# Four loops written out, the second batch's tokens fetched into idle buffers, and a last iteration that prepares nothing

## The reference

```
x = x + attn_a(layernorm(x), ...)   # 16 heads of 32, causal, biases on qkv and out
x = x + ffn(layernorm(x), ...)      # silu(x @ gate.T) * (x @ up.T) @ down.T, hidden 2048
x = x + attn_b(layernorm(x), ...)
x = x + ffn(layernorm(x), ...)
```

## Time and profile before

| | |
|---|---|
| median of 3 runs | 2034.46 us (2031.79 to 2035.56) |
| the profiled execution: its own time | 2035.76 us |
| its span, first to last instruction | 2034.0 us |
| instructions in the trace | 34492 |
| busy: PE, DVE, POOL, ACT | 1982.6, 1168.1, 999.4, 813.8 us |
| mean granted TensorE clock | 0.997 |

### The profile page before, as it was taken

The page is one execution under the profiler, slowest core; times in us unless marked ns, Lnnn a source line. Parts: engine busy times, 40 slices in busy tenths (PEclk is TensorE's granted clock), DMA queues, the critical chain, the costliest instruction groups (busy, mean ns, idle before and its releaser), DMA issues.

```text
span 2034.0 us, 34492 instructions
## 1 busy us (share of the span) xinstructions
PE 1982.6 (97%) x10304; PEld 1442.5 (71%) x10304; DVE 1168.1 (57%) x2404; ACT 813.8 (40%) x1481; POOL 999.4 (49%) x775
## 2 busy tenths in 40 slices
PE   7999999999999999999999999999999999999998
PEld 5555588888755558888765555888887555688887
DVE  4767555445577755454457775545456767544454
ACT  2388522221158742222115874222221676432221
POOL 4224359753312437975331243797533223389743
PEclk9999999999999999999999999999999999999999
DMA  4333111111333310111243331111113333111112
GB/s 150 90 79 90 33 42 54 51 63 42 85 75 85 74 43 32 62 53 52 73 136 75 85 75 43 32 63 52 52 43 85 74 84 75 43 42 63 53 53 83
DMA packets 59177, 134.07 MB, mean 66 GB/s; under 512 B 10720, under 2 KB 11744, under 8 KB 58976
## 3 DMA queue, kind: packets, MB, share of 16 engines
q1 hardware_dynamic: 58976, 131.66, 23.0%
HBM read 76.57 MB, written 4.19 MB: 40 GB/s over the span
## 4 chain that ended last, share of the span: by engine, by line
PE 89%; issue 3%; ACT 3%; DVE 2%; DMA 2%; POOL 0%; SPq 0%; DVEq 0%; ACTq 0%; POOLq 0%
PE bank L1306 11%; PE bank L1308 11%; PE bank L1307 11%; PE bank L1442 10%; PE ring L1306 10%; PE ring L1307 10%; PE ring L1308 10%; PE bank L1415 8%; PE ring L1384 7%; PE ring L1297 1%; ACT masked L831 1%; DMA area<-nm_lo 1%; ACT prob L809 1%; DMA x<-x_in 1%; DVE xn L1039 0%
## 5 line engine op out<-in xcount | busy, mean ns | idle before, releaser
L809 ACT ACTIVATE prob<-bank 128x512 f32<-128x512 f32 (+1 forms) x512 | 271.9, 571 | 143.5 <-PE bank L1415 115.1
L611 POOL TENSOR_SCALAR area<-w_stage 128x1024 fp32r<-128x1024 f32 x129 | 139.5, 1082 | 366.8 <-PE bank L1308 206.3
L688 POOL TENSOR_SCALAR_AFFINE_SELECT prob<-prob 128x512 f32<-128x512 f32 x128 | 82.9, 648 | 479.5 <-ACT prob L809 339.8
L613 POOL TENSOR_TENSOR area<-w_stage,area 128x1024 fp32r<-128x1024 f32 x129 | 309.2, 2397 | 10.8
L1110 DVE TENSOR_TENSOR x<-x,bank 128x512 f32<-128x512 f32 x256 | 171.1, 685 | 234.3 <-PE bank L1308 233.1
L1039 DVE CUSTOM_DVE_ANT_0 xn<-ring,mask_row 128x384 bf16<-128x384 f32 (+7 forms) x384 | 246.3, 661 | 86.7 <-PE ring L1384 84.4
L1306 PE MATMUL ring<-xt_hi,area 128*128 128x512 f32 x672 | 266.3, 396 | 1.6 <-DVE area L1143 1.0
L1307 PE MATMUL ring<-xt_lo,area 128*128 128x512 f32 x672 | 262.9, 391 | 0.0
L1308 PE MATMUL ring<-xt_hi,area 128*128 128x512 f32 x672 | 262.6, 391 | 0.0
L1415 PE MATMUL bank<-area 98*128 98x512 f32 (+3 forms) x768 | 247.8, 380 | 7.1 <-DMA area<-nm_lo 3.9
L1384 PE MATMUL ring<-area 96*128 96x512 f32 (+3 forms) x768 | 227.4, 362 | 9.9 <-DVE row_max L1039 5.5
(11 more groups left out here) (166 smaller groups left out, 3626.5 us busy)
## 6 DMA issues: line engine op xcount, KB each, us to landing
w_stage<-ffn_w SPq DMA_DIRECT2D x96, 512.0 KB, 3.3
area<-kq_parts SPq DMA_DIRECT2D x336, 128.0 KB, 2.3
w_stage<-attn_w SPq DMA_DIRECT2D x35, 512.0 KB, 3.3
area<-attn SPq DMA_DIRECT2D x48, 128.0 KB, 2.3
x<-x_in SPq DMA_DIRECT2D x20, 256.0 KB, 3.9
out<-x SPq DMA_DIRECT2D x16, 256.0 KB, 2.5
bias_rows<-row_bias SPq DMA_DIRECT2D x10, 256.0 KB, 4.4
area<-nm_hi SPq DMA_DIRECT2D x32, 8.0 KB, 1.8
```

Source lines behind the costliest of these rows:

```text
L611: pool.tensor_scalar(hi, src, 1.0, 0.0, ALU.mult, ALU.add).then_inc(w_hi_done, 1)
L613: pool.tensor_tensor(lo, src, hi.bitcast(F32), ALU.subtract).then_inc(w_split, 1)
L809: act.activation(prob[:, step % PROB_BUFS, h, off:], scores_at(u, j, h), ACT.Exp, scale=SCALE).then_inc(prob_ready, 1)
```

## The change

1. The loops over iterations are written out on all engines, so that every wait compares with a constant; `wait_alone` is gone, and each of its waits is a plain one, without the extra wait for `const_ready`.
2. Before it loads slot 18 of iteration 1, SP fetches all eight token tiles of the second batch into `masked` (six tiles) and `prob[:, 1]` (two tiles). The statistics and the normalisation of iteration 2's first layer norm read these copies. `x` itself is still reloaded behind the stores; POOL waits for it before it adds the output bias.
3. Iteration 3 loads no further weights or biases, reloads no `x`, and makes no statistics, transposes, splits or ones for a following iteration.

```diff
+LAST = BATCH * LAYERS - 1
+STAGE_BEFORE = 18
...
+        def staged_tile(t):
+
+            return masked[:, t // 2, t % 2 * DIM:(t % 2 + 1) * DIM] if t < 2 * MASKED_BUFS else prob[:, 1, t - 2 * MASKED_BUFS, :]
+
+        def first_layer(it):
+
+            return it % LAYERS == 0
+
+        def source_tile(it, t):
+
+            return staged_tile(t) if it and first_layer(it) else x[:, t, :]
...
-        def wait_alone(eng, semaphore, value):
...
+            def stage_x(it, batch):
+                sp.wait_ge(row_summed, it * SUM_TILES + SUM_TILES + MASKED_BUFS)
+                sp.wait_ge(pv_done, it * KEY_STEPS + KEY_STEPS)
+                for t in range(TT):
+                    sp.dma_start(staged_tile(t), x_in[batch, t * P:(t + 1) * P, :]).then_inc(x_staged[t // CT], 16)
...
-                with sp.Fori(0, LAYERS) as layer:
+                for layer in range(0, LAYERS):
...
+                    if it < LAST:
+                        sp.wait_ge(out_bias_added, it * TT + TT)
+                        load_biases(1 - layer)
+                    for i in range(12, SLOTS + (AHEAD if it < LAST else 0)):
+                        if i == STAGE_BEFORE and it < LAST and first_layer(it + 1):
+                            stage_x(it, b + 1)
...
-                        if n >= AFTER_STORE and not (b == BATCH - 1 and c):
+                        if n >= AFTER_STORE and b < BATCH - 1:
...
+                for s in x_loaded if first_layer(it) else ():
+                    pool.wait_ge(s, (it // LAYERS + 1) * (16 * CT))
...
-                wait_alone(pool, prob_ready, it * S2_STEPS + GH * (step + 1))
+                pool.wait_ge(prob_ready, it * S2_STEPS + GH * (step + 1))
...
+                if it == LAST:
+                    return
...
-                act.preload_act_table_set(EXP_TABLE)
-
-                xt_to_hi(it + 1, ("ln1", 0))
-                xt_to_hi(it + 1, ("ln1", 1))
+                if it < LAST:
+                    act.preload_act_table_set(EXP_TABLE)
+                    xt_to_hi(it + 1, ("ln1", 0))
+                    xt_to_hi(it + 1, ("ln1", 1))
...
+                if it == 0:
+                    dve.wait_ge(x_loaded[c], 16 * CT)
+                elif first_layer(it):
+                    dve.wait_ge(x_staged[c], it // LAYERS * (16 * CT))
                 for t in range(c * CT, (c + 1) * CT):
-                    tile_stats(t)
+                    tile_stats(t, source_tile(it, t))
...
-                dve.wait_ge(rows_drained, rows_taken(it, ROWS - CT - 1))
-                chunk_stats(it + 1, 0, b + layer + 1)
+                if it < LAST:
+                    dve.wait_ge(rows_drained, rows_taken(it, ROWS - CT - 1))
+                    chunk_stats(it + 1, 0)
...
-            with pe.Fori(0, BATCH * LAYERS) as it:
+            for it in range(BATCH * LAYERS):
                 iteration(it)
```

More of the change, by code:

```diff
@@ L310, in block_kernel @@
         x_loaded = [sem(f"x_loaded{c}") for c in range(CHUNKS)]
+        x_staged = [sem(f"x_staged{c}") for c in range(CHUNKS)]
         x_stored = [sem(f"x_stored{t}") for t in range(TT)]
@@ L495, in load_weights @@
                 if i >= 2 or it is not None:
-                    wait_alone(sp, w_split, (0 if it is None else it * SLOTS) + i - 1)
+                    sp.wait_ge(w_split, (0 if it is None else it * SLOTS) + i - 1)
                 j = i % SLOTS
@@ L598, in split_weights @@
                     if after[0] == "product":
-                        wait_alone(pool, product_full, products(it, *after[1:]))
+                        pool.wait_ge(product_full, products(it, *after[1:]))
                     elif after[0] == "rows":
-                        wait_alone(pool, rows_full, it * ROWS + after[1] + 1)
+                        pool.wait_ge(rows_full, it * ROWS + after[1] + 1)
                     elif after in SIDE:
-                        wait_alone(pool, side_full, side_done(it, after))
+                        pool.wait_ge(side_full, side_done(it, after))
                     else:
-                        wait_alone(pool, ring_full, full(it, after))
+                        pool.wait_ge(ring_full, full(it, after))
                 elif place(j) in LENT_PLACES:
                     lent_steps = KEY_STEPS if place(j) == 0 else J_BASE[6]
-                    wait_alone(pool, s2_full, it * S2_STEPS + GH * lent_steps)
+                    pool.wait_ge(s2_full, it * S2_STEPS + GH * lent_steps)
                 hi, lo, src = *w_part(j, slice(0, SLOT)), w_stage[:, j % 2, :]
@@ L722, in _, with iteration @@
                 split_weights(0, i)
-            with pool.Fori(0, BATCH * LAYERS) as it:
+            def iteration(it):
                 inverse_deviation(it, 0, 1)
@@ L750, in _ @@
                 inverse_deviation(it, 1, 1)
-                wait_alone(pool, xn_ready, it * 2 * TT + 2 * TT)
-                for i in range(FFN_SLOT0 + 3, SLOTS + 2):
+                pool.wait_ge(xn_ready, it * 2 * TT + 2 * TT)
+                for i in range(FFN_SLOT0 + 3, SLOTS + (2 if it < LAST else 0)):
                     if i == DIFFS_AT:
-                        wait_alone(pool, ring_drained, drained(it, ("ln2", 3)))
+                        pool.wait_ge(ring_drained, drained(it, ("ln2", 3)))
                         for n in range(6):
@@ L765, in _ @@
                     split_weights(it, i)
+            for it in range(BATCH * LAYERS):
+                iteration(it)
         @block.scalar
@@ L958, in _ @@
             xt_to_hi(0, ("ln1", 1))
-            with act.Fori(0, BATCH * LAYERS) as it:
+            for it in range(BATCH * LAYERS):
                 iteration(it)
@@ L1004, in xt_to_lo, with iteration @@
                 ins.then_inc(ring_drained, 1)
-            def iteration(it, b, layer):
+            def iteration(it):
                 def take_v(t):
@@ L1279, in _ @@
             xt_to_lo(0, 0, 1)
-            with dve.Fori(0, BATCH) as b:
-                with dve.Fori(0, LAYERS) as layer:
-                    iteration(b * LAYERS + layer, b, layer)
+            for it in range(BATCH * LAYERS):
+                iteration(it)
         @block.tensor
```

99 lines of the change are left out of this document (50 added, 49 removed).

## The result

The changed kernel takes 2010.95 us (median of 5 runs, 2009.98 to 2012.1), beside 2034.46 us for the kernel before (5 runs, 2031.79 to 2036.66): a ratio of 0.9887, 95% interval 0.9873 to 0.99, so 1.1% faster. The forecast was 2016.0 us in a range of 2010 to 2025. The sign and the range hold, and the gain is 23.5 us where 18.5 were worked out.

The account below looks back on a forecast made before the run. TensorE was taken as the bound, busy 1982.6 of 2034.0 us. Terms 8.3 + 5.4 + 0.8 + 4.0 = 18.5 us off the profiled 2035.8 give 2017.3, less 1.3 to the median: 2016.0 us, range 2010 to 2025.

Parts of the forecast that it names:

- The second boundary: Iteration boundary where the second batch starts: staged tokens take the `x` reload off the path, 8.3 us off (7.8 to 8.9).
- the cover that was named: POOL adds the output bias only behind slot 3's split; slot 18 lands with 2.7 us to spare: both cost nothing.
- The last iteration: End of iteration 3: without the stall, transposes and splits, the last addition ends some 6.3 us after gate and up, 5.4 off.
- The jumps: Loop branches at iteration boundaries: PE gains 0.8 us at the first and third; the middle one is in the 8.3.
- The waits: Hand-overs with constant wait values: maxima, SP and POOL gain, exponentials lose; 4 us off, bounds 9 off and 5 on.
- The maxima: DVE's row maxima: the wait for scores sits on the operation, 0.11 us sooner at 44 chain hand-overs, 4.8 us off.
- The exponentials: ACT's exponentials: the later of two waits is set apart, 0.06 us later at 20 chain hand-overs, 1.2 us on.
- The register instructions: Instructions for register values in the loops: not shown as PE's bound anywhere, so given nothing.
- the stacking on SP and POOL's masks: Split of the maxima and its copy on SP, 1.0 us off; POOL's masks, four times 0.1 us off.
- the waits give more: Rival: half of DVE's 162 waits for scores count fully, ACT pays nothing; 9 us off, 2009 to 2012 us; 9%.
- slower: Rival: the instruction set apart delays every exponential, at all 512 wide ones 31 us on, 2047 us; 4%.

Follow-up runs that it names:

- loops_plain: The kernel before with its loops written out and its waits in ordinary form, without token copies, last iteration still preparing a next one: 2022.79 us, ratio 0.9938.
- no_copies: The changed kernel without the early token fetches, iteration 2's first layer norm reading the reloaded `x` as before: 2018.8 us, ratio 0.9914.
- last_prepares: The changed kernel whose last iteration again makes all preparations for a next one, but with no reload of `x` ahead of them: 2013.45 us, ratio 0.9892.
- maxima_alone: The changed kernel with DVE's wait for the scores set apart again ahead of the row maxima: 2013.65 us, ratio 0.9894.
- loops_alone: The kernel before with only its loops written out; `wait_alone` stays, with constants as values: 2030.18 us, ratio 0.997.
- exps_again: The changed kernel with the two waits of each exponential exchanged, scores first and free buffer second: 2007.60 us, ratio 0.9869.

## Why the prediction was right, and where it was short

**The second boundary: right.** 8.3 us were worked out. 508.62 has become 497.43, 11.2 less, and the other two intervals fell by 2.9 on average, which leaves 8.2. By the matmuls it is 9.0, of which loops_plain shows 1.0 without the copies. no_copies gives 6.6 to 7.9 back, with the clock low for half as long in its profiled execution. POOL's wait for `x` and the fetch of the copies cost nothing, with the cover that was named.

**The last iteration: right.** 5.4 us were forecast and 5.35 measured, closer than the working earned: the last addition was put 6.3 us behind gate and up and is 6.57 behind, which makes 5.1, and the tail behind it, which was taken to stay as it was, gave 0.3. last_prepares splits the 5.1 into 2.1 and 3.0.

**The jumps: small, as the row on PE said.** 0.9 and 0.5 us, 1.4 together, at the first and third boundary against 0.8 for both; 3 × 3.31 us did not come. The Trainium skill ("Runtime: NRT & Kernel Launch", Instruction fetch mechanics) has every far taken branch stall until its page is fetched: DVE's gap of 3.31 us is gone with the branch, which agrees, and PE hid most of it.

**The waits: right in kind, too small by more than half.** The term was 4.0 us; the traces show 6.7 in attention and 3.4 in the seven-product step, 10.1 together, beyond even its bound of 9. Its parts:
- The maxima: 4.8 us before the 80%, and maxima_alone gives 4.3 by the matmuls. That the two are so close is partly luck, since the 44 pieces that were counted at 0.11 us are not of one form: 20 are a lone wait as at 57.74, 16 stand beside a register instruction, and in 8 only the 0.02 us is on the chain.
- The exponentials: +1.2 forecast, 2.8 to 3.8 measured. The chain of the kernel before had 20 such hand-overs, and the number that pays is about 55 (3.3, the middle of the two, divided by 0.06): the chain shows those that were last already, and not those that become last when each is later.
- The register instructions: "I give them nothing" is the sentence that failed. I looked for them at PE; they stood on DVE, among the 44 hand-overs that I had counted: 12 times between wait and maximum, at 0.15 us each beyond the lone wait, 1.8 us, and 4 times ahead of a wait. Attention's balance asks for more: 6.7 gained, 4.3 of it the maxima, and 3.3 lost on ACT leave 5.7 us for registers, the stacking on SP and POOL's masks, for which 1.4 was forecast. loops_alone, with registers gone and exponentials already late, gained 1.3 net, so the registers may be 4 to 5 of these. That division is argued from single executions and is not isolated.
- POOL's waits in its sums and weight splits: not looked for. Their rows were in the timeline of before (0.43 us of idle time between two sums), but POOL is busy 49% of the time, and I took its own lateness as harmless. It reaches PE through DVE's `diff_lo`.

The result lies in the band of the rival "the waits give more" (2009 to 2012 us), but its mechanism, in which ACT pays nothing, is refuted: exps_again shows that ACT does pay. That the time stayed inside the range, 1 us above its lower end, is partly luck: the waits' gain lay outside the bounds of its own term. In the rival "slower" one step is wrong: 2047 us starts from the forecast of 2016.0 us, in which the waits have gained 4.0 us already, and not from the 14.5 us of the other terms, which would make it 2051. By medians the parts nearly close: 2035.64 less 5.5 (loops) and 7.4 (form of the waits) is loops_plain's 2022.8; less 7.9 (copies), 2.5 (the last iteration's work) and 2.1 (the wait for its reload) it is 2010.3, beside 2010.95.

## What to carry to other kernels

Where an instruction has two waits, name first the one that usually comes last: the first stays on the instruction, the second is set apart, and exchanging two lines on ACT was worth 2.6 us here. When a change shortens many hand-overs, count them in PE's waits for the engine and not only in the chain of waits, and look at which operation of another engine stretches beside one that now ends earlier, as DVE's `diff_lo` did beside POOL. Here a loop whose values sit in registers cost more at the hand-overs of the engine that computes them than at the jump, by the division argued above.

## What the runs showed of the hardware

- From the releasing event to the start of the operation, by the medians in the traces of before, after and exps_again, a wait on the operation took 0.02 us on DVE and ACT, 0.06 to 0.08 on POOL and 0.02 on SP's transfers; set apart it took 0.13 on DVE, 0.08 on ACT, 0.12 to 0.15 on POOL and 0.06 on SP. The price of one lone wait is thus 0.11, 0.06, 0.07 and 0.05 us.
- Two executions of the changed kernel differ by 2.7 us up to the first scores, some 47 us in: 2.0 by when PE's clock rises, 0.6 by when its first matmul starts.
- In all five kernels of the table above `diff_lo` ends 1.08 us after POOL's operation, and DVE took 2.07 to 3.04 us for the same work, according to how late POOL was.
